# Turning round the second product of a feed-forward: weights stationary, 512 tokens moving

## The reference, cut to what matters

```python
# x: (2, 1024, 256)
x = x + (mha(ln(x, g1, be1), ln(x, g1, be1), causal=True) @ W1 + b1)
x = x + (mha(ln(x, g2, be2), ctx, causal=False) @ W2 + b2)
xn3 = ln(x, g3, be3)
x = x + relu(xn3 @ Wf1 + bf1) @ Wf2 + bf2      # Wf1: 256 x 1024, Wf2: 1024 x 256
```

## Time and profile before

| | us |
|---|---|
| median of 3 runs | 626.71 |
| lowest and highest run | 624.55 and 627.41 |
| profiled execution, span from first to last instruction | 631.5 |

### The profile page before, as it was taken

The page is one execution under the profiler, slowest core; times in us unless marked ns, Lnnn a source line. Parts: engine busy times, 40 slices in busy tenths (PEclk is TensorE's granted clock), DMA queues, the critical chain, the costliest instruction groups (busy, mean ns, idle before and its releaser), DMA issues.

```text
span 631.5 us, 8807 instructions
## 1 busy us (share of the span) xinstructions
PE 504.7 (80%) x3296; PEld 296.2 (47%) x3296; DVE 368.2 (58%) x695; ACT 307.5 (49%) x590; POOL 187.8 (30%) x276
## 2 busy tenths in 40 slices
PE   1775775999997999799988835669576757989887
PEld 0664452344443444344333333434222446988877
DVE  4887697678886788678532147645221763454430
ACT  3544020667765776477666502247443535253460
POOL 3788821131221132122132523305131350121200
PEclk9988697799999999899999969767555968999998
DMA  8138936007367335727260266978333212101001
GB/s 288 47 109 158 201 116 118 0 21 116 52 120 105 67 66 107 115 56 38 83 186 1 68 168 92 173 108 140 107 99 115 81 47 72 34 0 34 18 17 34
DMA packets 41930, 56.51 MB, mean 89 GB/s; under 512 B 12832, under 2 KB 27424, under 8 KB 41888
## 3 DMA queue, kind: packets, MB, share of 16 engines
q1 hardware_dynamic: 39584, 47.56, 38.1%
q10 hardware_dynamic: 2304, 8.39, 3.8%
HBM read 35.12 MB, written 20.42 MB: 88 GB/s over the span
## 4 chain that ended last, share of the span: by engine, by line
PE 44%; DMA 23%; DVE 15%; ACT 6%; SPq 5%; issue 3%; POOL 2%; ACTq 0%; DVEq 0%
PE ps L864 10%; PE ps L973 9%; PE ps L948 8%; PE ps L911 7%; DMA arena_h<-heads 6%; DMA stacks<-shift_t 6%; PE ps L1060 5%; DMA recips<-recip_rows 4%; DVE max_a L1141 4%; ACT arena_p L732 4%; DMA heads<-out_t 4%; DVE xn L1094 3%; SPq L409 2%; PE ps L933 2%; SPq L428 2%
## 5 line engine op out<-in xcount | busy, mean ns | idle before, releaser
L732 ACT ACTIVATE arena_p<-ps 128x512 f32<-128x512 f32 (+4 forms) x416 | 190.9, 541 | 129.5 <-PE ps L948 127.3
L1141 DVE TENSOR_REDUCE max_a<-ps 128x1 f32<-128x512 f32 (+4 forms) x280 | 159.6, 620 | 46.6 <-PE ps L911 34.0
L948 PE MATMUL ps<-stacks 99*128 99x512 bf16 (+2 forms) x448 | 149.9, 369 | 27.6 <-DMA stacks<-shift_t 22.5
L911 PE MATMUL ps<-stacks 96*128 96x77 bf16 (+4 forms) x640 | 146.2, 306 | 32.1 <-DVE max_a L1141 19.1
L911 PEld LDWEIGHTS ps<-stacks 96*128 96x128 bf16 x640 | 58.9, 111 | 97.5 <-DVE max_a L1141 45.5
L973 PE MATMUL ps<-arena_p,v_group 128*32 128x512 f32 (+4 forms) x896 | 94.1, 540 | 0.7 <-POOL arena_p L617 0.5
L617 POOL TENSOR_SCALAR_AFFINE_SELECT arena_p<-arena_p 128x512 f32<-128x512 f32 x64 | 41.0, 653 | 169.9 <-ACT arena_p L732 169.9
L948 PEld LDWEIGHTS ps<-stacks 99*128 99x128 bf16 (+1 forms) x448 | 45.6, 107 | 93.1 <-ACT arena_p L732 37.8
L1141 DVE TENSOR_REDUCE max_b<-ps 128x1 f32<-128x384 f32 (+3 forms) x88 | 52.5, 636 | 21.3 <-PE ps L915 21.3
L864 PE MATMUL ps<-wf2r,hid_r 128*128 128x256 f32 x384 | 49.9, 294 | 9.6 <-DVE hid_r L1254 9.6
L864 PEld LDWEIGHTS ps<-wf2r,hid_r 128*128 128x128 f32 x384 | 49.1, 202 | 10.7 <-DVE hid_r L1254 10.7
(11 more groups left out here) (68 smaller groups left out, 528.1 us busy)
## 6 DMA issues: line engine op xcount, KB each, us to landing
heads<-out_t ACTq DMA_DIRECT2D x16, 512.0 KB, 4.3
stacks<-q_parts SPq DMA_DIRECT2D x48, 128.0 KB, 5.2
stacks<-k_parts SPq DMA_DIRECT2D x48, 128.0 KB, 7.6
stacks<-qc_parts SPq DMA_DIRECT2D x48, 128.0 KB, 5.1
arena_h<-heads SPq DMA_DIRECT2D x8, 512.0 KB
recips<-recip_rows SPq DMA_DIRECT2D x8, 512.0 KB
q_parts<-parts SPq DMA_DIRECT2D x8, 384.0 KB, 2.5
k_parts<-parts SPq DMA_DIRECT2D x8, 384.0 KB, 2.6
```

Source lines behind the costliest of these rows:

```text
L732: nc.scalar.activation(probs[0:a.kp, a.probs_slot(g, ui), h, k * BANK:k * BANK + width], ps[0:a.kp, unit % S_BANKS, 0:width], ACT.Exp, sca ...
L911: ins = nc.tensor.matmul(m_bank(use)[:, o:o + w], q_stack[0:ROWS, g % a.nb, h, t * P:(t + 1) * P], k_rows(ROWS, g, h, s0, s0 + w), start=T ...
L948: ins = nc.tensor.matmul(ps[0:keys, unit % S_BANKS, lo - k * BANK:hi - k * BANK], k_rows(ROWS_S, g, h, i * P, i * P + keys), q_stack[:, g ...
L1141: nc.vector.tensor_reduce(dst, m_bank(use)[:, 0:nh * w].rearrange("p (h w) -> p h w", h=nh), AX.X, ALU.max).then_inc(s.max_read, 1)
```

## The change

The second product is computed transposed. For each of two blocks c of 128 output channels, 24 matmuls have a 128x128 block of `wf2r` stationary and the chunk's 512 tokens of `hid_r` moving, into bank 6 (c = 0) or 7 (c = 1). ScalarE copies each bank into `ff_t`, which reuses the place of `out_t` (`copy_ff`). TensorE transposes the copies back into banks 6 and 7, eight transposes of 128x128 (`turn_out`), and VectorE adds those to `xs`. The transposes of chunk n stand after the first two blocks f of chunk n+1's first product, for the last chunk after its second product. The residual product of the chunk after next follows behind these transposes. VectorE takes two low halves of the new chunk, then the addition of the chunk before, then the residual product's addition and sums, two more low halves, the normalisation and the last four.

```diff
--- before.py
+++ after.py
@@ -295,6 +295,7 @@
 
 
 
+        ff_t = out_t[:, :].rearrange("p (c t) -> p c t", c=KC)
         acc = ps[:, 6:8, :].rearrange("p b (j c) -> p (b j) c", c=C)
         out_region = ps[:, 6:8, :].rearrange("p b n -> p (b n)")
 
@@ -346,7 +347,7 @@
 
         a_order = [("v", n) for n in range(NCH)] + [("vc", 0)] + [("w", NCH + n) for n in range(2, NCH)]
         for n in range(NCH):
-            a_order.append(("f", n))
+            a_order += [("ft", n), ("f", n)]
             if n + 2 < NCH:
                 a_order.append(("w", 2 * NCH + n + 2))
         a_at = {key: i for i, key in enumerate(a_order)}
@@ -791,7 +792,7 @@
             def hidden(n):
 
                 if n:
-                    act.wait_ge(acc_full, 2 * a_at["f", n - 1] + 2)
+                    act.wait_ge(acc_full, 2 * a_at["ft", n - 1] + 2)
                 for f in range(FF // P):
                     u = U_H + n * (FF // P) + f
                     act.wait_ge(ring_full, u + 1)
@@ -801,10 +802,23 @@
                     nc.scalar.activation(full[:, u % 2, :], ps[:, 2 + u % 4, :], ACT.Relu,
                                          bias=col[:, BF1 + f:BF1 + f + 1]).then_inc(hid_done, 1)
 
+            def copy_ff(n):
+
+                i = a_at["ft", n]
+                if n == 0:
+                    act.wait_ge(S2.heads_stored, 16 * NG)
+                else:
+                    act.wait_ge(acc_full, 2 * a_at["f", n - 1] + 2)
+                for c in range(KC):
+                    act.wait_ge(acc_full, 2 * i + c + 1)
+                    nc.scalar.activation(ff_t[:, c, :], ps[:, 6 + c, :], ACT.Copy).then_inc(acc_read, 1)
+
             for n in range(NCH):
                 if n:
                     copy_norm(2 * NCH + n)
+                    copy_ff(n - 1)
                 hidden(n)
+            copy_ff(NCH - 1)
 
 
         @block.tensor
@@ -1042,17 +1056,32 @@
 
             def feed_out(n):
                 pe.wait_ge(hid_low, (FF // P) * (n + 1))
+                i = a_at["ft", n]
                 if n == 0:
                     pe.wait_ge(wf2_halves, 2)
                     pe.wait_ge(S2.out_copied, NG)
-                terms = [(k, hw, hx) for k in range(FF // P) for hx, hw in PASSES]
-                rows_product(("f", n), lambda t, j: hid_r[:, terms[t][2], terms[t][0], j * P:(j + 1) * P],
-                             lambda t: wf2r[:, terms[t][1], terms[t][0], :], len(terms))
-
-            def hidden(n):
+                terms = [(k, hw, hx) for k in range(FF // P) for hw, hx in PASSES]
+                for c in range(KC):
+                    pe.wait_ge(acc_read, 2 * (i - 1) + c + 1)
+                    for t, (k, hw, hx) in enumerate(terms):
+                        ins = nc.tensor.matmul(ps[:, 6 + c, :], wf2r[:, hw, k, c * P:(c + 1) * P], hid_r[:, hx, k, :],
+                                               start=(t == 0), stop=(t == len(terms) - 1))
+                    ins.then_inc(acc_full, 1)
+
+            def turn_out(n):
+
+                pe.wait_ge(acc_read, 2 * a_at["f", n])
+                for half in range(2):
+                    for j in (2 * half, 2 * half + 1):
+                        for c in range(KC):
+                            ins = nc.tensor.transpose(acc[:, j, c * P:(c + 1) * P], ff_t[:, c, j * P:(j + 1) * P],
+                                                      identf[:, :])
+                    ins.then_inc(acc_full, 1)
+
+            def hidden(n, fs):
                 k = 2 * NCH + n
                 pe.wait_ge(xn_low, KC * (n + 1))
-                for f in range(FF // P):
+                for f in fs:
                     u = U_H + n * (FF // P) + f
                     ring_free(u)
                     terms = [(kc, hw, hx) for kc in range(KC) for hw, hx in PASSES]
@@ -1064,12 +1093,16 @@
 
             for n in range(NCH):
 
-                hidden(n)
+                hidden(n, range(0, 2))
+                if n:
+                    turn_out(n - 1)
+                if n and n + 1 < NCH:
+                    heads_product(2 * NCH + n + 1, S2, W2)
+                hidden(n, range(2, FF // P))
                 if n + 1 < NCH:
                     turn_norm(2 * NCH + n + 1)
                 feed_out(n)
-                if n + 2 < NCH:
-                    heads_product(2 * NCH + n + 2, S2, W2)
+            turn_out(NCH - 1)
 
 
         @block.vector
@@ -1266,18 +1299,20 @@
                     invert_sums(NG - 1)
                     hidden_low_halves(n, range(4, FF // P))
                     divide_heads(NG - 1)
-                elif n + 1 < NCH:
-
-                    add_rows(("w", 2 * NCH + n + 1), n + 1, NCH + n + 1)
-                    ln_sums(2 * NCH + n + 1)
-                    hidden_low_halves(n, range(0, 4))
-                    ln_apply(2 * NCH + n + 1)
+                else:
+                    hidden_low_halves(n, range(0, 2))
+                    add_rows(("f", n - 1), n - 1, 2 * NCH + n - 1)
+                    if n + 1 < NCH:
+
+                        add_rows(("w", 2 * NCH + n + 1), n + 1, NCH + n + 1)
+                        ln_sums(2 * NCH + n + 1)
+                    hidden_low_halves(n, range(2, 4))
+                    if n + 1 < NCH:
+                        ln_apply(2 * NCH + n + 1)
                     hidden_low_halves(n, range(4, FF // P))
-                else:
-                    hidden_low_halves(n, range(FF // P))
                 if n + 1 < NCH:
                     xn_low_half(n + 1)
-                add_rows(("f", n), n, 2 * NCH + n)
+            add_rows(("f", NCH - 1), NCH - 1, 3 * NCH - 1)
 
 
 def kernel(x, ctx_1024, **w):
```

## The result

The changed kernel takes 638.33 us (median of 4 runs, 636.7 to 640.85) where the kernel before takes 627.06 (4 runs, 624.55 to 630.32). The ratio is 1.0151, 95% interval 1.0105 to 1.0197, that is 6.6 to 12.4 us slower. Timed again twice, the ratio was 1.009 (1.0052 to 1.0128) and 1.0161 (1.0101 to 1.0221). About 7 us lies in all three intervals. Medians here are over all runs and ratios over fast runs alone, those within 1.5% of the fastest of their kernel; the profiled runs of heads_back and fine_after were slower than that, so only stretches of them are compared. The profiled execution has a span of 636.4 us.

What follows compares the result with a forecast made beforehand. TensorE was taken to bound the feed-forward nearly throughout. The terms -1.6 + 3.1 + 3.8 + 1.5 + 2.0 + 0.2 gave +9.0 us, 635.7 us on the median of 626.71, range 631 to 639.5.

Steps and rivals of the forecast that it cites:

- the product itself: Second product, four chunks: 11.20 us each at the first product's price instead of 11.61, 1.6 us saved.
- transposes and wait, chunks 1 and 2: Before the moved residual product: transposes of 1.03 us, then TensorE idle 1.89 us for VectorE's addition, twice; +5.9 us.
- transposes, chunk 3: Eight transposes back among chunk 3's first product, on TensorE's path; +1.0 us.
- tail and stores: After the last matmul: copy, transposes and two additions instead of one, +2.0 us; stores closer together, +0.2.
- clock behind the new gaps: After the new idles in chunks 1 and 2: TensorE's clock falls behind one of two, +1.5 us; bounds 0 to 3.0.
- The move and its wait: Residual product moved behind the transposes in chunks 1 and 2: TensorE waits 1.89 us for VectorE's addition, twice; +3.8 us.
- Weight loads as the bound: Rival, second product: halved weight loads set its pace, 5.8 us a product, 614.1 us in all; chance 0.04.
- A covered wait: Rival, before the residual product: VectorE's low halves come early enough, no idle or clock fall; +3.7, 630.4 us; chance 0.06.
- late low halves: Rival, before second products: VectorE late with remaining low halves, plus both clock falls and serial stores; +14, 640.7 us; chance 0.06.

Runs made afterwards that it cites:

- heads_back: Changed kernel with the residual product put back directly behind the second product, its copies on their own semaphore; median 632.84 us, ratio 1.0005 to the kernel before.
- fine_after: Changed kernel with the second product's wait split by low halves instead of waiting for all eight; median 624.93 us, ratio 0.9867 to the kernel before.
- add_first: Changed kernel, but VectorE adds the chunk before behind one low half of the new chunk instead of two; median 633.93 us, ratio 1.004.
- double_turn: Changed kernel with every transpose back done twice, 64 in place of 32, result unchanged; median 637.56 us, ratio 1.0128.
- half_width: Changed kernel with 256 instead of 512 tokens moving in each matmul of the second product, weights still stationary; median 640.34 us, ratio 1.0145.
- tail_rows: Changed kernel, but the last chunk's second product is done in rows as before, nothing copied or turned back; median 634.89 us, ratio 1.01.

## Why the prediction was right, step by step

| term | predicted, us | profile after, us | from |
|---|---|---|---|
| the product itself | -1.6 | -2.4 | 4 x (11.61 - 11.02) |
| transposes and wait, chunks 1 and 2 | +5.9 | +6.0 | end of one second product to the next: 17.31 to 20.32, twice |
| transposes, chunk 3 | +1.0 | +0.9 | 13.44 to 14.31 |
| tail and stores | +2.2 | +2.2 | 3.29 to 5.45 |
| clock behind the new gaps | +1.5 | 0 | both residual products at 1.00 |
| sum | +9.0 | +6.7 | +7.1 from the first second product on; the falls in the first and last product differ by 0.4 |

The time of 638.33 lies in the range of 631 to 639.5, 2.6 us above the 635.7 given. That agreement is partly luck. Without falls the profiles differ by 6.7 us, so the sum of 9.0 was 2.3 too high: 1.5 for a clock that did not fall and 0.7 for the product. The first four runs against four came out at 11.3, above both.

*The move and its wait* was the step that carried the forecast, and it was right in mechanism and size: idle 1.90 us where 1.89 was worked out, released by VectorE's addition. It was worked out from the second low half ending 4.99 us after the first product's start, and after the change it ends just there (546.16 against 541.17). From the residual product's start to the next second product 14.5 us were kept; it is 14.6. heads_back takes the idle away by moving the residual product back, add_first takes 1.33 of 1.90 us away by the order on VectorE alone, and both return what that costs. One thing the sum had differently: it priced the transposes and the wait as two terms. double_turn shows that in chunks 1 and 2 only their sum is set, by VectorE; free transposes would then mean a longer idle and not a shorter time, but that was not run.

*The product* was mis-sized by 0.7 us. The price of the first product, 0.2333 us, was too high; the turned product runs at 0.2296. Why two products of the same shape differ by 1.6% no run shows. half_width shows that the saving of 0.59 us a product is the width of the moving operand alone.

*The clock* term was not borne out in the profile after. Over the profiles with an idle of 1.90 us before the residual product (changed kernel, two repeats, tail_rows, half_width, fine_after) it fell behind 3 of 12 gaps: once in half_width and twice in fine_after, where the residual product takes 5.38 us. In the three profiles of the changed kernel itself it fell behind none of 6. The price of 1.5 us was near (1.7), the chance of one in two too high for an average; for one execution the forecast can't be better than such a share. One of its bounds was misread: the last product's 13.26 us run to its modelled end and stand against 11.77, so that fall cost 1.49 us and not 1.65. From the Trainium skill's statement on transposes ("TensorE: Matmul & The Clock Gate", Part 4: PE-mode transpose) the prediction worked out that both gaps would fall; the runs do not bear that out, since 9 of 12 did not. The other gaps speak against it too: 1.03 us of transposes and 1.63 of idle were followed by a fall in 0 of 18 cases, 2.08 us of idle straight behind matmuls in 4 of 9. Were transposes as quiet as idle, the first would be the longer pause. The two gaps also stand in different places, so this is a sign, not an isolation.

*The tail* was right: 5.45 - 3.29 = 2.2 us, and tail_rows brings it back to 3.3. The 0.2 of it for the stores was not isolated.

*The rivals.* Weight loads as the bound would have given 5.8 us a product; they fill 8.93 of 11.02 us after the change and the product is 5% shorter. Nor do these matmuls run at the Trainium skill's 131 ns for 512 columns ("TensorE: Matmul & The Clock Gate", Back-to-back issue gap): here it is 230 ns. A covered wait and late low halves did not occur; the gaps before the second products stayed at 1.63 and 2.08 us.

## What to carry to other kernels

Halving the number of matmuls by widening the moving operand saved 5% of the product here; the columns streamed, 24576 either way, stayed the same, and the time nearly with them. That saving, 0.59 us, did not pay for turning the result back, which cost 0.87 us a chunk where it was on TensorE's path without a wait (chunk 3). Before moving a step among other work, look at the queue of the engine that must free its buffers: here an addition placed behind two unrelated low halves left TensorE idle for 1.90 us, longer than the 1.03 us that the transposes themselves took. And where an engine waits for the last of many pieces, let it start on the first: one wait split into eight gave 2%, more than the change took.

## What the runs showed of the hardware

The granted clock behind one and the same gap is not the same in each execution. Behind the idle of 2.08 us before the last second product it fell in the kernel before, the changed kernel, half_width and tail_rows and held in the two repeats, heads_back, add_first and double_turn. Behind 1.90 us it fell 3 times in 12, behind 1.63 us never in 18 gaps of nine profiles, both with 1.03 us of transposes ahead of the idle. Before the first second product, also behind transposes, it fell in the eight profiles with an idle of 3.26 to 4.32 us and held in the first repeat with 2.63. A fall costs 1.3 to 1.7 us, so profiles of one kernel differ by up to 3 us in this stretch alone (107.85, 106.36 and 104.73 us from the first second product to the end).
